# Token sums in four 32-row quarters with a bank and a copy each, and two chunks of the first layer kept on chip

## The reference, cut to what matters

```python
# x [10000,512], 5000 edges (src, dst) with 64 attributes each
n   = layernorm(x)
msg = relu(n[src] + edge_attr @ W_e + b_e)
agg = segment_sum(msg, dst)
h   = (1 + eps) * n + agg
h   = silu(batchnorm(h @ W1 + b1))      # [10000,1024], statistics over all 10000 rows
h   = silu(batchnorm(h @ W2 + b2))      # [10000, 512]
x   = x + h
y   = layernorm(x)                      # groups g of 16 tokens t, 16 experts e x 4 sets s
logits = einsum('gtd,des->gtes', y, controller) + tie
perm   = (logits == max over t)         # picks one token of each group for each (e, s)
inter  = einsum('gtd,desf->gtesf', y, f1)
inner  = relu(einsum('gtesf,gtes->gesf', inter, perm))
inter2 = einsum('gesf,esfd->gesd', inner, f2)
out = x + einsum('gesd,gtes->gtd', inter2, perm)
```

## Time and profile before

| | us |
|---|---|
| median of 3 runs | 1946.03 (1945.61 to 1946.71) |
| the profiled execution, its own time | 1943.54 |
| its span | 1941.8 |
| busy PE, DVE, ACT, POOL | 1814.2, 1184.6, 988.8, 364.1 |
| from the start to the first layer | 0 to 226 |
| first layer | 226 to 696 |
| handover to the second layer | 696 to 706 |
| second layer | 706 to 1147 |
| mixture | 1147 to 1942 |

### The profile page before, as it was taken

One profiled execution on the slowest core, in us unless ns is written; L12 is line 12 of the kernel. 1 busy time (PEld: TensorE's weight loads), 2 busy tenths in 40 slices (PEclk: granted clock), 3 DMA queues, 4 the chain that ended last, 5 costly groups with the idle time before them and its releaser, 6 DMA issues. The chain is left out here.

```text
span 1941.8 us, 40638 instructions
## 1 busy us (share of the span) xinstructions
PE 1814.2 (93%) x15580; PEld 1315.7 (68%) x15580; DVE 1184.6 (61%) x2341; ACT 988.8 (51%) x1716; POOL 364.1 (19%) x386
## 2 busy tenths in 40 slices
PE   5587699999999989999999987999999999999999
PEld 3354578888888878888888876565665665665654
DVE  6488466666666543333333336777778777777766
ACT  2355123333333356665566525667667667666653
POOL 4486320000000000000000014223222223222210
PEclk9777899999999999999999999999999999999999
DMA  9987756566566464433344237445455545455432
GB/s 366 304 170 109 172 170 169 169 169 169 169 177 181 141 264 146 163 136 127 129 159 155 84 112 235 135 141 161 134 144 156 145 140 158 135 152 158 126 89 86
DMA packets 209216, 310.81 MB, mean 160 GB/s; under 512 B 57234, under 2 KB 133970, under 8 KB 205875
## 3 DMA queue, kind: packets, MB, share of 16 engines
q1 hardware_dynamic: 200111, 287.84, 48.0%
q0 software_dynamic: 8960, 20.98, 5.6%
HBM read 171.31 MB, written 137.46 MB: 159 GB/s over the span
## 5 line engine op out<-in xcount | busy, mean ns | idle before, releaser
L1546 PE MATMUL bank<-f2s,inner_bd 128*32 128x512 f32 x2528 | 295.8, 596 | 0.6 <-DVE inner_bd L1149 0.5
L1445 ACT ACTIVATE inter_hi<-bank 128x512 fp32r<-128x512 f32 x316 | 189.2, 599 | 177.1 <-PE bank L1546 176.2
L599 ACT ACTIVATE h1o<-bank,b_by_channel 128x500 f32<-128x500 f32 x160 | 108.5, 678 | 324.6 <-PE bank L431 316.1
L1367 DVE TENSOR_TENSOR inter_lo<-bank,inter_hi 128x512 fp32r<-128x512 f32 x316 | 214.5, 688 | 57.6 <-ACT inter_hi L1445 53.1
L429 PE MATMUL bank<-hhi,w_hi 128*128 128x500 f32 x624 | 244.5, 392 | 0.0
L431 PE MATMUL bank<-hhi,w_lo 128*128 128x500 f32 x624 | 243.6, 390 | 0.0
L430 PE MATMUL bank<-hlo,w_hi 128*128 128x500 f32 x624 | 242.5, 389 | 0.0
L429 PE MATMUL bank<-ahi,w_hi 128*128 128x500 f32 x608 | 237.3, 390 | 0.0
L430 PE MATMUL bank<-alo,w_hi 128*128 128x500 f32 x608 | 236.6, 389 | 0.0
L431 PE MATMUL bank<-ahi,w_lo 128*128 128x500 f32 x608 | 236.4, 389 | 0.0
L563 DVE BATCH_NORM_STATS2 stats<-h1o 128x500 f32 (+1 forms) x160 | 103.2, 675 | 155.5 <-ACT h1o L599 155.5
(11 more groups left out here) (141 smaller groups left out, 3261.9 us busy)
## 6 DMA issues: line engine op xcount, KB each, us to landing
h1T<-h1o SPq DMA_DIRECT2D x19, 2000.0 KB, 8.1
h1in<-h1T SPq DMA_DIRECT2D x19, 2000.0 KB, 9.7
aggregate<-at SPq DMA_DIRECT2D x20, 1024.0 KB
x<-in_x SPq DMA_DIRECT2D x79, 256.0 KB, 2.9
x<-x SPq DMA_DIRECT2D x79, 256.0 KB, 3.6
x_back<-x SPq DMA_DIRECT2D x79, 256.0 KB, 3.0
out<-x_back SPq DMA_DIRECT2D x79, 256.0 KB, 2.2
h2in<-h2T SPq DMA_DIRECT2D x39, 512.0 KB, 4.1
```

What stands on the lines that cost most here:

```text
L599: nc.scalar.activation(h1o[b][:, m, :], mb[m % 4][:, 0:CW], ACT.Identity, bias=b1c[:, m:m + 1]).then_inc(evr, 1)
L1367: nc.vector.tensor_tensor(ilo[b][:, :], bI[b][:, :], ihi[b][:, :].bitcast(F32), ALU.subtract).then_inc(ilr, 1)
L1445: nc.scalar.activation(ihi[b][:, :], bI[b][:, :], ACT.Copy).then_inc(ihr, 1)
L1546: last = nc.tensor.matmul(bI[b][32 * i:32 * i + 32, :], ibd[:, e, j, :, :].rearrange("p s g -> p (s g)"), f2s[:, e, :], start=True, stop=True)
```

## The change

`sums` now works in four quarters of 32 rows (32 tokens, 2 groups), so that `GH` is 2 and the mask operand has 64 x 2 = 128 columns. Each quarter writes all four channel chunks into one bank of its own: quarters 0 to 3 into `bD[1]`, `bD[0]`, `bI[0]`, `bI[1]`, in a crossing tile into `bI[0]`, `bI[1]`, `bD[0]`, `bD[1]`. Outside of crossings the four quarters run side by side and both waits stand ahead of the first product; in a crossing quarters 0 and 1 come first and then 2 and 3. There are still four copies of 512 elements, now one a quarter, with runs of 2 elements in `yT` instead of 4. `final` waits for one copy instead of two.

The last two chunks of the first layer are no longer stored: `h1o` of `gnn_up` and the input buffers of `gnn_down` are the same memory, which in `edge_aggregate` holds the gathered rows. `gnn_down` takes these two chunks first and the other 18 after them, by `columns(c)`. PE does 26 warming products at the end of `gnn_up` and 8 instead of 20 at the start of `gnn_down`.

```diff
-GH = GB // 2
+QR = 4
+GH = GB // QR
-HP = P // 2
+HP = P // QR
@@ edge_aggregate
-        xg = sb("xg", [P, XW * EW, H])
+        xg = first["rows"]
@@ gnn_up
-        h1o = [sb(f"h1o{i}", [P, KF, CW]) for i in range(2)]
-                store(NCH - 2, 0)
-                for m in range(0, KF, 2):
-
-                    sp.wait_ge(evr, (NCH - 1) * KF + m + 2)
-                    sp.dma_start(h1T[m:m + 2, :, span(NCH - 1)].rearrange("m p n -> p m n"), h1o[1][:, m:m + 2, :])\
-                        .then_inc(stl, 16)
-                sp.wait_ge(sto[0], 16 * (NCH // 2))
-                sp.wait_ge(sto[1], 16 * (NCH // 2 - 1))
-                sp.wait_ge(stl, 16 * (KF // 2))
+                for b in range(2):
+                    sp.wait_ge(sto[b], 16 * (NCH // 2 - 1))
                 multiply(NCH - 1, 1, 0, KF)
+                keep_clock(nc, tb[0], ident, 26)
@@ gnn_down
-        h1 = [sb(f"h1in{i}", [P, KF, CW]) for i in range(2)]
+                def columns(c):
+
+                    return span(c + NCH - 2 if static(c, 2) else c - 2)
+
                 def load(c, b):
-                    if not static(c, 2):
-                        sp.wait_ge(hir, (c - 1) * KF)
-                    sp.dma_start(h1[b][:, :, :], h1T[:, :, span(c)].rearrange("m p n -> p m n")).then_inc(ldh[b], 16)
+                    sp.wait_ge(hir, (c - 1) * KF)
+                    sp.dma_start(h1[b][:, :, :], h1T[:, :, columns(c)].rearrange("m p n -> p m n")).then_inc(ldh[b], 16)
-                for i in range(PIECES):
-                    ks = slice(i * KF // PIECES, (i + 1) * KF // PIECES)
-                    sp.dma_start(h1[0][:, ks, :], h1T[ks, :, span(0)].rearrange("m p n -> p m n")).then_inc(ldp[i], 16)
-                load(1, 1)
                 for k in range(KH):
                     sp.dma_start(f1s[:, k, :], f1[k * P:(k + 1) * P].rearrange("p e s f -> p (e s f)")).then_inc(wf1, 16)
-                with sp.Fori(0, NCH // 2 - 1) as it:
+                load(2, 0)
+                store(0, 0)
+                load(3, 1)
+                store(1, 1)
+                with sp.Fori(1, NCH // 2 - 1) as it:
                     load(it * 2 + 2, 0)
                     store(it * 2, 0)
-                sp.wait_ge(sto[0], 16)
+                sp.wait_ge(sto[0], 32)
-                        keep_clock(nc, psum[7], ident, 20)
+                        keep_clock(nc, psum[7], ident, 8)
@@ mixture
-        bY, bF = [bD, bI[0:2]], bD[1]
-        def bank_pairs(kb, j):
-
-            return bY[::-1] if crossing(kb, j) else bY
+        bY, bF = [bD[1], bD[0], bI[0], bI[1]], bD[1]
+        def sum_banks(kb, j):
+
+            return [bI[0], bI[1], bD[0], bD[1]] if crossing(kb, j) else bY
-                def to_yT(k, kb, j, c, r):
+                def to_yT(k, kb, j, r):
                     t = k * TB + j
-                    act.wait_ge(yp, t * KH + c + r + 1)
-                    nc.scalar.activation(yT[:, c:c + 2, :, j * GB + r * GH:j * GB + (r + 1) * GH],
-                                         bank_pairs(kb, j)[c // 2][r][:, :].rearrange("p (c e g) -> p c e g", c=2, g=GH), ACT.Copy).then_inc(yr, 1)
+                    act.wait_ge(yp, t * QR + r + 1)
+                    nc.scalar.activation(yT[:, :, :, j * GB + r * GH:j * GB + (r + 1) * GH],
+                                         sum_banks(kb, j)[r][:, :].rearrange("p (c e g) -> p c e g", c=KH, g=GH), ACT.Copy).then_inc(yr, 1)
-                    for h, pair in enumerate(bank_pairs(kb, j)):
-                        if kb is not None and pair is bD and not static(kb * TB + j, 1):
+                    banks = sum_banks(kb, j)
+                    for together in ((0, 1), (2, 3)) if crossing(kb, j) else (range(QR),):
+                        if kb is not None and bF in [banks[r] for r in together] and not static(kb * TB + j, 1):
                             pe.wait_ge(otr, kb * TB + j)
-                        if kb is not None and pair is not bD:
+                        if kb is not None and bI[0] in [banks[r] for r in together]:
                             pe.wait_ge(ilr, lows(kb, j - 1 if crossing(kb, j) else j, 1))
                         done = {}
-                        for c in (2 * h, 2 * h + 1):
+                        for c in range(KH):
                             for part in (xhi, xlo):
-                                for r in range(2):
+                                for r in together:
                                     rows = slice(r * HP, (r + 1) * HP)
                                     done[r] = nc.tensor.matmul(
-                                        pair[r][:, (c % 2) * HP * GH:(c % 2 + 1) * HP * GH],
+                                        banks[r][:, c * ES * GH:(c + 1) * ES * GH],
                                         part[j % 2][rows, c * P:(c + 1) * P],
                                         pbd[rows, j % 2, :, :].rearrange("p e g -> p (e g)"), start=part is xhi, stop=part is xlo)
-                        for r in range(2):
+                        for r in together:
                             done[r].then_inc(yp, 1)
-                    copied = KH if crossing(kb, j) else 2
+                    copied = KH if crossing(kb, j) else 1
@@ gnn_mixture
+            rows_h1 = second.enter_context(nc.sbuf_tensor("rows_or_h1", [P, 4 * EW * H], F32))
+            h1 = [rows_h1[:, i * KF * CW:(i + 1) * KF * CW].rearrange("p (m n) -> p m n", m=KF) for i in range(2)]
+                chunk["rows"] = rows_h1[:, :].rearrange("p (t h) -> p t h", h=H)
...
```

More of the change, by code:

```diff
@@ L432, in product, with gnn_up @@
     return last
-def gnn_up(nc, sem, psum, ident, mhalf, x, agg, w1, vec, h1T, stats1, W2, w2, first, norm):
+def gnn_up(nc, sem, psum, ident, mhalf, x, agg, w1, vec, h1T, h1o, stats1, W2, w2, first, norm):
     with ExitStack() as ctx:
@@ L454, in gnn_up @@
         lda = [sem(f"agg_chunk_loaded{i}") for i in range(2)]
-        stl = sem("h1_last_stored")
         sto = [sem(f"h1_stored{i}") for i in range(2)]
@@ L699, in norm_finish, with gnn_down @@
     dve.wait_ge(norm["shr"], 1)
-def gnn_down(nc, sem, psum, ident, mhalf, h1T, vec, w2, h2T, stats2, norm, norm2, f1, f1s, wf1, h2first, ldh2):
+def gnn_down(nc, sem, psum, ident, mhalf, h1T, h1, vec, w2, h2T, stats2, norm, norm2, f1, f1s, wf1, h2first, ldh2):
     with ExitStack() as ctx:
@@ L714, in gnn_down @@
         h2o = [sb(f"h2o{i}", [P, KH, CW]) for i in range(2)]
-        PIECES = 4
-        ldp = [sem(f"h1_first_loaded{i}") for i in range(PIECES)]
         ldh = [sem(f"h1_loaded{i}") for i in range(2)]
@@ L770, in _ @@
                     sp.wait_ge(evr, (NCH - 1) * KH + m + 1)
-                    sp.dma_start(h2T[m, :, span(NCH - 1)], h2o[1][:, m, :]).then_inc(stl, 16)
+                    sp.dma_start(h2T[m, :, columns(NCH - 1)], h2o[1][:, m, :]).then_inc(stl, 16)
                 sp.wait_ge(sto[0], 16 * (NCH // 2))
@@ L813, in nonlinear @@
                 def nonlinear(c, b):
-                    if not static(c, 1):
-                        act.wait_ge(ldh[b], half(c, b, 16) - (16 if b == 0 else 0))
                     if not static(c, 2):
+                        act.wait_ge(ldh[b], half(c, b, 16) - 16)
                         act.wait_ge(mmr, (c - 1) * KH)
@@ L1435, in body @@
                                 act.wait_ge(inp, k * QB)
-                            for c in range(0, KH, 2):
-                                for r in range(2):
-                                    if kb is not None or c + r < KH - 1:
-                                        to_yT(k, kb, n, c, r)
+                            for r in range(QR if kb is not None else QR - 1):
+                                to_yT(k, kb, n, r)
                         if what == "unit":
@@ L1701, in gnn_mixture @@
                 chunk = first_buffers(first, f1s)
+                chunk["rows"] = rows_h1[:, :].rearrange("p (t h) -> p t h", h=H)
                 edge_aggregate(nc, sem, psum, ident, x, src, dst, edge_attr, W_e, b_e, agg, W1, w1, vectors, vec, w2, chunk)
-                gnn_up(nc, sem, psum, ident, mhalf, x, agg, w1, vec, h1T, stats1, W2, w2, chunk, norm1)
-            gnn_down(nc, sem, psum, ident, mhalf, h1T, vec, w2, h2T, stats2, norm1, norm2, f1, f1s, wf1, h2first, ldh)
+                gnn_up(nc, sem, psum, ident, mhalf, x, agg, w1, vec, h1T, h1, stats1, W2, w2, chunk, norm1)
+            gnn_down(nc, sem, psum, ident, mhalf, h1T, h1, vec, w2, h2T, stats2, norm1, norm2, f1, f1s, wf1, h2first, ldh)
         mixture(nc, sem, psum, ident, mhalf, x, h2T, x1d, seld, controller, f1s, f2, out, stats2, norm2, wf1, h2first, ldh)
```

13 lines of the change are left out of this document (5 added, 8 removed).

## The result

| | before | after |
|---|---|---|
| median of the runs on one chip | 1943.89 us (20 runs, 1938.34 to 1947.98) | 1948.18 us (20 runs, 1945.96 to 1952.43) |
| ratio, 95% interval | | 1.0024 (1.0017 to 1.0031) |
| the profiled execution, its own time | 1943.54 | 1952.43 |
| its span | 1941.8 | 1950.7 |
| mean granted clock, profiled execution | 0.974 | 0.970 |

A forecast was written before the change was run, and what follows sets the result against it. TensorE, busy 93% of the span, was taken to bound the kernel, except at the handover and partly in the first block. Terms -7.6 + 1.1 + 3.1 + 1.0 - 2.8 = -5.2 took 1946.0 to 1940.8 us; range 1930 to 1957.

The forecast's parts named there:

- First block: Mixture's first eight tiles: four odd tiles -0.12 us each, four even ones +0.37 each from later copies; sum +1.0 us.
- handover: Between the two layers: ACT needs no DMA for the first chunk, so the second layer's first product comes earlier; -2.8 us.
- plain tiles: Sums of 63 mixture tiles outside first block and crossings: 1.025 us with a load-bound step of 0.11, -0.12 each, -7.6 us.
- wait moved to the front: On 27 even tiles the sums wait for DVE's low part before their first product; 0.04 us each, +1.1 us.
- copies to `yT`: ACT's copies of the sums start about 0.35 us later, covered in plain tiles; shorter written runs not charged; 0.
- crossing tiles: Eight tiles whose quarters go in two passes: sums of 1.905 us instead of 1.52, 0.39 each, +3.1 us.
- a step of 0.12: Rival for the sums' rounds: the step stays 0.12 us, total 1946.7 us; chance 0.25 together with gains taken back.
- halved sums: Rival for the sums: weights fetched early enough, rounds stream-bound at 0.065 us, -26.5 us, total 1914; chance 0.10.
- loads in twos: Rival for the sums: four quarters' weight loads run only two at a time, +54 us, about 2000; chance 0.10.
- rival 4: DVE's low part or the copies take back what PE gains in the sums; about 1947 us; chance 0.25 with unchanged step.

The follow-up runs named there:

- half the channels: The changed kernel with weights of 64 instead of 128 channels from the second block on, half of the sums left out; 1926.04 us, one run.
- half the mask: The changed kernel with products of 64 instead of 128 mask columns from the second block on, half of the sums left out; 1943.79 us, one run.
- two passes: The changed kernel with the mixture's first block taking its quarter sums in two passes of two quarters; 1949.32 us (12 runs), ratio 1.0017.

## Why the prediction was wrong

The direction was wrong. The step that failed is **First block** (+1.0 us, measured +9.0), with the sentence in the handover's part that nothing is added for the clock, which weighed the clock at that one place only. It made a loss of what would have been about even: with more warming in the first block the changed kernel came to 0.9999. What was missing for the forecast gain beside it are the fetches (+2.9), which are in no step. By its own steps:

| step | forecast | measured |
|---|---|---|
| plain tiles | 63 x -0.12 = -7.6 | 63 x -0.105 (1.044 against about 1.15) = -6.6 |
| wait moved to the front | 27 x 0.04 = +1.1 | 27 x 0.08 = +2.2 |
| copies to `yT` | 0 | 28 ns longer, no new wait at `final` |
| crossing tiles | 8 x 0.39 = +3.1 | 8 x 0.37 = +3.0 |
| first block | +1.0 | +9.0 |
| handover | -2.8 | -2.85 |
| fetches behind the first block | not in it | +2.9 |

- **The pace of the sums** was right: 1.04 to 1.05 against 1.025, a load-bound step of 0.112 for the 0.11 taken. The parts erred against each other, a first step of 0.17 for 0.22 and a tail of 0.21 for 0.145. The rivals of a step of 0.12, of halved sums and of loads in twos are out by this step; the run with half the channels shows besides that the loads went four at a time, and that only narrower loads made them faster.
- **The wait in front** was at 0.04 with a bound of 0.07 and is 0.08. The term was mis-sized; the place and the even tiles alone were right. A start of 0.05 behind the low part was taken, and the sums began 0.16 behind it (1478.55 for 1478.39). Together with it the steady stage gained 2.15 of the 3.2 that the terms give for it (62 tiles of -0.12, +1.1 and +3.1). Of these 2.15, 1.3 go with where the fetches fall and not with the sums: idle time without a releaser is 1.8 us in that stage after and 3.1 before. Without it the gain is about 0.9, where the terms as measured give 1.3.
- **The handover** was right in size and in cause.
- **The first block** was worked out at the full clock, since the profile before had it there. At the full clock the step holds: with more warming in both kernels the difference is 1.5 us, for 1.0. What failed is that the clock was taken as given. The row was at hand: among the waits before, PE idles four times for 1.6 us there, between warming products that keep the clock, and I lengthened that idle time by 0.37 each without asking what the clock would do. Of the five kernels with the changed kernel's first block and the old warming, four have 0.82 in the block's profile (after, its repetition, quarters only, half the channels) and one has 0.90 (half the mask); two passes have 0.94; every kernel with halves there has 0.97 to 1.00. It is not the one profiled execution: over all the timed runs the mean granted clock of the whole kernel was 0.9701 after (20 runs), 0.9697 in the repetition (11) and 0.9676 with quarters only (5), against 0.9735 before (35), 0.9744 with halves in the first block and the crossings (11) and 0.9740 in the changed kernel with more warming (11). The difference of 0.0034 between before and after is 2 x 0.0034 x 1948 = 13 us more at 1.2 GHz. Before, 3.4 us at 1.2 GHz lie in the handover (granted clock 0.83 over the 10 us from 696 to 706, and 1.00 after), which the change takes away, so that about 17 us came in elsewhere, against 21 in the profiled first block.
- **The fetches** were in no step. Of a step that is moved, I counted the instructions that it issues by their time, 0.11 a load, and not by what they shift: 56 instructions 500 us ahead of a place made that place 2 to 3 us longer, and so the kept chunks alone brought nothing.

What rival 4 (nothing but the handover counts) said of the size, +1 us, was nearer than the forecast, by other causes than its own: neither DVE's low part nor the copies took the gain back.

**Left open.** Which property of the quarters lets the clock fall, the idle span of 2.1 instead of 1.6 us or the narrower sums before it, was not separated: two passes lengthened the sums as well as changing what runs side by side. The length of the span does not decide alone. With two passes PE's four waits before L1459 are back at 1.6 us (6.5 in all, for 6.4 before), and the clock still was at 0.50 from 1170.0 to 1173.4 and from 1183.6 to 1187.0; with halves and the same 1.6 us it stayed up in three kernels (1.00) and fell once in three others (0.97 to 0.98), in two of them only at the block's end. Why quarters alone (1.0043) cost more than quarters with kept chunks (1.0024), when the chunks alone bring nothing, is partly the clock (0.9676 against 0.9701, of which the handover's 3.4 us are 0.0009), and why it differs is not known. The three profiled stages where the changed kernel is a bit longer (before the first layer, the mixture's start, the end; 1.7 us together) vary by as much among the others (before the first layer 214.55 to 218.67 us) and have no cause shown. The profile's difference of 8.9 us against 4.3 us between the medians is such scatter in part; how much of the fall a typical execution has is only known from the mean clock.

## What to carry to other kernels

Where an engine has slack and its clock is held up by filler, an edit's price is not only its own time but what the clock makes of the idle time: look at the granted clock of each short stretch that the edit touches, and keep the old form there if it only pays in the steady part. Splitting a product by rows gives only as much as its weight loads allow: halve the mask and the round stays, halve the loaded channels and it halves. Before crediting an edit early in a program, compare the gaps without a releaser in the dense stretches behind it, and try the edit with the old number of instructions.

## What the runs showed of the hardware

- Four 32-row loads of 128 channels run together, 0.112 us a round, with 128 or 64 streamed columns; 0.06 us with 64 channels.
- Idle spans of PE grown from 1.6 to 2.1 us, with narrower sums ahead of them, went with 21 us at the 1.2 GHz level in a stage that had been at 2.4 throughout. The stage became 9.0 us longer, and 104 more products without use brought 6.7 of it back.
- Where 16 ns products with a load each run through the program, idle time without a releaser of 0.2 to 2.1 us stands at places 127 products (254 instructions) apart, fixed by the number of instructions before them. A 16 KB packet of instruction fetches (110 for 1.80 MB) lands 1.2 to 1.7 us before such a gap ends. A shift of 56 instructions cost or gave 1.8 to 2.9 us in that stage.
- Copies from a bank in runs of 2 elements took 631 ns, in runs of 4 or whole rows 603 and 599.
